# Expert rows added onto preset residual rows by the scatter DMA, and a final stage that reads one row per token in place of two

## The reference, cut to what matters

```python
x = _layernorm(x + _L0_attn_ref(x, ...), axis=-1)
x = _layernorm(x + _L0_xattn_ref(x, ctx_1024, _lenS2, ...), axis=-1)      # x2
x = _layernorm(x + _L0_ffn_ref(x, ...), axis=-1)

# _L0_ffn_ref
probs = jax.nn.softmax(xf @ router_w.T, axis=-1)
topv, topi = jax.lax.top_k(probs, 2)
probs = probs * mask                       # mask: 1 at topi, else 0
probs = probs / (probs.sum(axis=-1, keepdims=True) + 1e-09)
h = jax.nn.silu(g) * u                     # g, u: xf @ gate_w[e] + gate_b[e], xf @ up_w[e] + up_b[e]
expert_out = jnp.einsum('nef,efd->ned', h, down_w) + down_b
y = jnp.einsum('ne,ned->nd', probs, expert_out)
```

## Time and profile before

| What | us |
|---|---|
| median of 3 runs | 1800.53 |
| the profiled execution's own time | 1800.48 |
| its span (first to last instruction) | 1798.6 |
| expert stage's loop, first to last scatter issue | 1345.3 to 1748.7 |
| final stage, first load to last store's issue | 1756.0 to 1794.5 |

### The profile page before, as it was taken

The page is one execution under the profiler, slowest core; times in us unless marked ns, Lnnn a source line. Parts: engine busy times, 40 slices in busy tenths (PEclk is TensorE's granted clock), DMA queues, the critical chain, the costliest instruction groups (busy, mean ns, idle before and its releaser), DMA issues. The chain is left out here.

```text
span 1798.6 us, 30884 instructions
## 1 busy us (share of the span) xinstructions
PE 1530.3 (85%) x10698; PEld 1085.6 (60%) x10698; DVE 1113.7 (62%) x2342; ACT 744.4 (41%) x1630; POOL 660.0 (37%) x571
## 2 busy tenths in 40 slices
PE   6998982389999999985899999997559999999970
PEld 3554542378888888652677777776426666666650
DVE  5898892457777775560557777778525545555545
ACT  5666651024434443462555455452113333333324
POOL 1645435413223330100343565655423333333320
PEclk9998995579999999998999999999669999999995
DMA  3242326655556545143123113103301111111117
GB/s 101 82 163 82 135 110 141 166 120 131 135 144 162 150 121 178 58 154 129 56 82 106 44 60 126 36 25 106 141 21 45 45 48 46 45 48 45 48 36 280
DMA packets 188843, 177.73 MB, mean 99 GB/s; under 512 B 88359, under 2 KB 147419, under 8 KB 188571
## 3 DMA queue, kind: packets, MB, share of 16 engines
q1 hardware_dynamic: 174075, 148.70, 27.9%
q0 software_dynamic: 10400, 22.95, 3.9%
q10 hardware_dynamic: 4224, 4.19, 0.7%
HBM read 115.68 MB, written 60.11 MB: 98 GB/s over the span
## 5 line engine op out<-in xcount | busy, mean ns | idle before, releaser
L599 DVE SCALAR_TENSOR_TENSOR conv_y<-conv_in,taps,conv_y 128x512 f32<-128x512 f32 x192 | 184.2, 977 | 30.0 <-ACT conv_y L464 25.4
L2341 POOL DMA_INDIRECT y<-o,idx x71 | 83.3, 1173 | 242.0 <-DVE o L2484 234.2
L2420 ACT ACTIVATE xsT<-pX 128x256 f32<-128x256 f32 x71 | 27.2, 383 | 304.0 <-PE pX L2365 304.0
L2376 PE MATMUL pG<-w_gu,xsT 128*128 x284 | 135.5, 600 | 1.2 <-ACT xsT L2420 1.1
L2376 PE MATMUL pU<-w_gu,xsT 128*128 x284 | 134.7, 597 | 0.0
L2397 PE MATMUL pD<-late,hT 128*128 x568 | 134.2, 379 | 0.0
L1792 PE MATMUL xQ<-late,last 128*128 128x512 f32 x256 | 124.9, 610 | 8.9 <-ACT late L1948 4.8
L379 PE MATMUL ps_j<-xnT,w_qkv 128*128 128x512 f32 x256 | 128.7, 639 | 0.0
L1747 POOL TENSOR_TENSOR sc<-sc,den 128x1232 f32<-128x1232 f32 x32 | 72.0, 2249 | 109.2 <-DVE den L2168 109.1
L2397 PEld LDWEIGHTS pD<-late,hT 128*128 128x128 f32 x568 | 102.5, 190 | 11.0
L2480 DVE TENSOR_TENSOR o<-pD,late 128x256 f32<-128x256 f32 x71 | 30.2, 425 | 121.5 <-PE pD L2397 121.5
(11 more groups left out here) (338 smaller groups left out, 3640.8 us busy)
## 6 DMA issues: line engine op xcount, KB each, us to landing
qkvg<-tok SPq DMA_DIRECT2D x8, 2048.0 KB, 6.6
qkvg<-gate SPq DMA_DIRECT2D x8, 1024.0 KB, 9.0
steps<-step SPq DMA_DIRECT2D x32, 256.0 KB, 4.3
qks<-qkvg SPq DMA_DIRECT2D x32, 256.0 KB, 4.7
vb<-qkvg SPq DMA_DIRECT2D x32, 256.0 KB, 4.7
gt<-qkvg SPq DMA_DIRECT2D x32, 256.0 KB, 3.3
y<-y SPq DMA_DIRECT2D x16, 512.0 KB, 8.0
vw<-even SPq DMA_DIRECT2D x4, 1232.0 KB
```

The costliest lines, as they stand in the source:

```text
L599: y = nc.vector.scalar_tensor_tensor(conv_y[m % 4][:], conv_in[b][:, m, k:k + BT], taps[:, m, k:k + 1], conv_y[m % 4][:], ALU.mult, ALU.add)
L2341: nc.gpsimd.indirect_dma_start(out=s["y"].rearrange("t p d -> (t p) d"), out_offset=bass.IndirectOffsetOnAxis(ap=idx[j % 8][:, 0:1], axis= ...
L2376: mm = pe.matmul(to[:], xsT[q][:, c, :], w_gu[:, bass.ds(e, 1), c, k * FF:(k + 1) * FF], start=c == 0, stop=c == KD - 1)
```

## The change

A token's two expert rows go to the same row of `y`, which beforehand holds the residual. The scatter is issued with `compute_op=ALU.add`, so the DMA adds what it carries to what memory holds. The residual is put there in cross_stage by a second store of each x2 block. `kept` goes, with its ACT instruction and its semaphore, and DVE's last operation on `o` becomes a tensor_scalar. The entries of the padding get spare rows of their own, one for each expert, list tile and partition. The final stage loads one tile per block, has a buffer for each block, and needs no sum. Lines not shown change names, counts of semaphores, or remove the flag.

```diff
+SPARE = (NE * (P - 1) + NE * REGION + P - 1) // P
@@ delta_stage, SP and POOL
-                    sp.wait_ge(blank_set, 3)
+                    sp.wait_ge(blank_set, NE + 3)
...
-                    nc.gpsimd.tensor_scalar(blank[:, :, 1], con[:, C_COL:C_COL + 1].broadcast_to([P, NE * REGION]),
-                                            float(2 * TILES * P), None, ALU.add).then_inc(blank_set, 1)
+                    for e in range(NE):
+                        nc.gpsimd.tensor_scalar(blank[:, e * REGION:(e + 1) * REGION, 1],
+                                                con[:, C_COL:C_COL + 1].broadcast_to([P, REGION]), float(NE),
+                                                float(TILES * P + e * REGION), ALU.mult, ALU.add).then_inc(blank_set, 1)
...
+                    pool.wait_ge(blank_set, NE + 2)
+                    spare = blank[:, :, 1].rearrange("p (e n) -> p e n", e=NE)
+                    nc.gpsimd.tensor_tensor(spare, spare, con[:, C_IOTA:C_IOTA + REGION].unsqueeze(1).broadcast_to(
+                        [P, NE, REGION]), ALU.add).then_inc(blank_set, 1)
@@ cross_stage
+                sp.dma_start(y_v[n], x2t[:]).then_inc(x2_out, 16)
...
-            nc.gpsimd.memset(ent[:, :, 0, 3], 1.0).then_inc(set_up, 1)
...
-                                            float((k * TILES + t) * P), None, ALU.add).then_inc(set_up, 1)
+                                            float(t * P), None, ALU.add).then_inc(set_up, 1)
...
-                        dve.wait_ge(x2_out, n * 16)
+                        dve.wait_ge(x2_out, n * 32)
@@ expert_stage, POOL
-                    pool.wait_ge(kept_done, j - 3)
...
-                    in_=o[q][:], in_offset=None).then_inc(o_out[q], 16)
+                    in_=o[q][:], in_offset=None, compute_op=ALU.add).then_inc(o_out[q], 16)
@@ expert_stage, ACT
-            def residual(j):
-                if j >= 4:
-                    act.wait_ge(o_done, j - 3)
-                act.wait_ge(xs_in[j % 4], 16 * (j // 4) + 16)
-                nc.scalar.activation(kept[j % 4][:], xs[j % 4][:], ACT.Copy, scale=rows[j % 8][:, 3:4]
-                                     ).then_inc(kept_done, 1)
@@ expert_stage, DVE
-                dve.wait_ge(kept_done, j + 1)
                 dve.wait_ge(ob_done, j + 1)
-                nc.vector.scalar_tensor_tensor(o[r][:], o[r][:], rows[j % 8][:, 0:1], kept[r][:], ALU.mult, ALU.add
-                                               ).then_inc(o_done, 1)
+                nc.vector.tensor_scalar(o[r][:], o[r][:], rows[j % 8][:, 0:1], None, ALU.mult).then_inc(o_done, 1)
@@ final_stage
-        y = [sb(f"y7_{q}", [P, 2, BLK, D]) for q in range(4)]
-        z = [sb(f"z7_{q}", [P, BLK, D]) for q in N]
+        y = [sb(f"y7_{q}", [P, BLK, D]) for q in N]
...
-                if n >= 4:
-                    sp.wait_ge(z_sum, n - 3)
-                for k in range(2):
-                    sp.dma_start(y[n % 4][:, k], y_v[k, n]).then_inc(y_in[n], 16)
+                sp.dma_start(y[n][:], y_v[n]).then_inc(y_in[n], 16)
...
-                dve.wait_ge(y_in[n], 32)
-                nc.vector.tensor_tensor(z[n][:], y[n % 4][:, 0], y[n % 4][:, 1], ALU.add).then_inc(z_sum, 1)
-                dve.wait_ge(z_sum, n + 1)
+                dve.wait_ge(y_in[n], 16)
@@ build
-        "y": dram("y", [2 * TILES + 1, P, D]),
+        "y": dram("y", [TILES + SPARE, P, D]),
```

More of the change, by code:

```diff
@@ L1589, in cross_stage @@
         x2_v = s["x2"].rearrange("(n t) p d -> n p t d", t=BLK)
+        y_v = s["y"][0:TILES].rearrange("(n t) p d -> n p t d", t=BLK)
         con = s["con"]
@@ L1652, in cross_stage @@
         RIDE = 4 * KC + 8
-        SET_UP = 5 + 3 * BLK + NE + 1
+        SET_UP = 4 + 3 * BLK + NE + 1
         JOBS = {0: (3, 4, 5), 1: (6, 7), 2: (0,), 3: (1, 2)}
@@ L1705, in _ @@
             store_x2(BLOCKS - 1)
-            sp.wait_ge(x2_out, 16 * BLOCKS)
+            sp.wait_ge(x2_out, 32 * BLOCKS)
         @block.gpsimd
@@ L2295, in expert_stage @@
         hT = [sb(f"hT6_{q}", [P, FK, P]) for q in Q]
-        kept = [sb(f"kept6_{q}", [P, D]) for q in R]
         o = [sb(f"o6_{q}", [P, D]) for q in R]
@@ L2304, in expert_stage @@
         o_out = [sem(f"e_o_out{q}") for q in R]
-        (idx_done, xT_done, xT_sb, gu_done, gb_done, ub_done, silu_done, h_done, hT_done, hT_sb, d_done, kept_done,
-         ob_done, o_done) = [
+        (idx_done, xT_done, xT_sb, gu_done, gb_done, ub_done, silu_done, h_done, hT_done, hT_sb, d_done, ob_done, o_done) = [
             sem(f"e_{n}") for n in ("idx_done xT_done xT_sb gu_done gb_done ub_done silu_done h_done hT_done hT_sb "
-                                    "d_done kept_done ob_done o_done").split()]
+                                    "d_done ob_done o_done").split()]
         block = ctx.enter_context(nc.Block())
@@ L2448, in _ @@
                     silu(j)
-                    residual(j)
         @block.vector
@@ L2518, in final_stage @@
         y_in = sems("y_in")
-        set_up, st_done, mv_done, sd_done, r_done, sh_done, z_sum, z_done, z_out = [
-            sem(f"f_{n}") for n in "set_up st_done mv_done sd_done r_done sh_done z_sum z_done z_out".split()]
-        y_v = s["y"][0:2 * TILES].rearrange("(k n t) p d -> k n p t d", k=2, t=BLK)
+        set_up, st_done, mv_done, sd_done, r_done, sh_done, z_done, z_out = [
+            sem(f"f_{n}") for n in "set_up st_done mv_done sd_done r_done sh_done z_done z_out".split()]
+        y_v = s["y"][0:TILES].rearrange("(n t) p d -> n p t d", t=BLK)
         out_v = out.rearrange("b (c t p) d -> (b c) p t d", p=P, t=BLK)
@@ L2544, in finish @@
                 for t in T:
-                    last = nc.scalar.activation(z[n][:, t, :], z[n][:, t, :], ACT.Identity, bias=shift[n][:, t:t + 1],
+                    last = nc.scalar.activation(y[n][:, t, :], y[n][:, t, :], ACT.Identity, bias=shift[n][:, t:t + 1],
                                                 scale=rstd[n][:, t:t + 1])
@@ L2548, in finish @@
                 act.wait_ge(z_done, n + 1)
-                act.dma_start(out_v[n], z[n][:]).then_inc(z_out, 16)
+                act.dma_start(out_v[n], y[n][:]).then_inc(z_out, 16)
             for n in N:
@@ L2567, in _ @@
             for n in N:
-                dve.wait_ge(y_in[n], 32)
-                nc.vector.tensor_tensor(z[n][:], y[n % 4][:, 0], y[n % 4][:, 1], ALU.add).then_inc(z_sum, 1)
-                dve.wait_ge(z_sum, n + 1)
+                dve.wait_ge(y_in[n], 16)
                 for t in T:
-                    nc.vector.bn_stats(stats[n][:, t, :], z[n][:, t, :]).then_inc(st_done, 1)
+                    nc.vector.bn_stats(stats[n][:, t, :], y[n][:, t, :]).then_inc(st_done, 1)
                 dve.wait_ge(st_done, n * BLK + BLK)
```

## The result

The changed kernel took 1793.19 us in the median of 17 runs, the kernel before 1802.16 us in the median of 17 runs beside them. The ratio is 0.9949, with a 95% interval of 0.9936 to 0.9962. Timed again on another occasion, the same two kernels gave 0.9967 (0.9953 to 0.9981). The profiled execution has a span of 1790.0 us against 1798.6 us.

The account below looks back on a forecast made before the run. PE was taken to bound the expert loop, the order of waits the final stage. From 1800.48 us, -9.3 us (final stage) and +2.5 us (last scatters) gave 1793.7 us, range 1789.5 to 1799 us.

Parts of the forecast that it names:

- The final stage: Final stage: without the sums and second loads, the last store is issued 9.3 us earlier, with ACT as the bound.
- The scatter's x: Expert stage: additional time of a scatter that adds in memory, between 0 and 2.8 us, taken as 1.0 us.
- The three landings in a row: End of the expert loop: the last three scatters move the stage's end by 3x - 0.54, +2.5 us at x = 1.0.
- The rule of the Trainium skill: Adding scatter: an adding DMA needs two source reads on one ring, delivering about half the bytes; x about 1.0 us.
- No cost in the loop: Expert loop: PE stays full, the period stays 5.81 us, and x is hidden up to 1.96 us.
- No cost of the second store, the blank list and the lost work of ACT and DVE: Cross stage, delta stage and expert loop: added stores, POOL's list work and removed ACT and DVE work count 0.
- A sign of being wrong: Delta or cross stage: a shift by more than 1 us was to show that the prediction is wrong.
- the third rival: Adding scatter: x is about 0, 9.3 + 0.5 us at most off, 1790.6 us; chance 0.10.
- The sum: Whole kernel: -9.3 us from the final stage and +2.5 us from the tail, together -6.8 us.

Follow-up runs that it names:

- the doubled scatter: The changed kernel with each adding scatter issued twice, the second after the first has landed; one run, 2002.7 us.
- The halves: The kernel before with only the new final stage, ratio 0.9943; the changed kernel with the old final stage (two loads and DVE's sum), ratio 1.0011.

## Why the prediction was right, step by step

- **The final stage** was forecast at -9.3 us and gave -7.9 and -9.2 us in the two profiles of the changed kernel, and -9.7 us alone. By the means of four profiles each, 39.2 us before and 29.5 us with one row per token, it is -9.7 us. The start was right (7.8 us behind the first load, forecast 7.6), the distance a little pessimistic (2.72, forecast 2.83). What the step left out is that a store's issue can stand behind the loads: 2.24 us in one profile, 1.00 in the other. I had counted 0.43 us for each.
- **The scatter's x**, the additional time of an adding scatter, was taken as 1.0 us, from the moving part of the scatter and the gather. In the tail of the first profile it came out as 1.25 us in the first distance (5.10 against 3.85), 0.54 us in the second (4.39) and 0.7 us in the last landing (3.8 against 3.1), 0.83 us in the mean, and 0.6 us of it is POOL's longer issue. In the loop the median landing grew by 1.4 us, from 2.6 to 4.0 us, which the loop's period hid.
- **The three landings in a row** were to cost 3x - 0.54 = 2.5 us. In the first pair of profiles they cost 2.1 us: 8.07 us from the first to the last of the three scatters became 9.49, and the landing adds 0.7. But the base was not a fixed one. I took 3.85 us as what two plain scatters in a row need, and with plain scatters the first distance was 5.2 to 5.6 us in three of five profiles. By the means the three scatters went from 8.7 to 9.2 us apart and the last landing from 3.0 to 3.7 us, so this part cost 1.2 us and was forecast at twice that.
- **The drain** was missing. I wrote that the end of the stage moves by 3x - 0.54 and took what follows the landing as fixed; it grew by 1.4 us. This is the step that failed. That the tail still cost about what was forecast (2.6 us by the means, 2.5 forecast; 3.5 us in the first pair of profiles) is luck: the missing drain made up for the landings that were priced too high.
- **The rule of the Trainium skill** ("Collectives: The Full Stack", "The bandwidth ceiling: the fold count and why AG ≠ RS ≠ AR") is stated there for the reduce step of a collective over several cores, and no run here shows that case. Its direction holds for this scatter: the DMA engines' share in the loop rose from 0.15 to 0.29 at 46 GB/s, about twice the engine time for the same counted bytes. The additional reads are not among these bytes: the page of the profile shows 111.5 MB read from memory after and 115.7 MB before, and the 4.2 MB less are the eight loads. The time from issue to landing grew less than the engine time did, by 0.7 us of 3.1 for the last scatter and by 1.4 us of 2.6 in the loop.
- **No cost in the loop**: right, with a period of 5.81 us. The forecast put the distance at 3.85 + 1.0 = 4.85 us; the doubled scatter shows 4.3 us, so of the 5.81 us 1.5 us were left.
- **No cost of the second store, the blank list and the lost work of ACT and DVE**: the store alone measured 1.0001. For the list, POOL's operations ended 0.9 us after 726.72, before SP's issue at 728.66. From the first of these operations to SP's issue it is 5.81 us, and was 5.80 us before:

```profile
722.85 2.56 POOL L990 TENSOR_SCALAR blank<-con 128x33 f32<-128x33 f32 x8
725.48 1.16 POOL L993 TENSOR_SCALAR blank<-con 128x264 f32<-128x264 f32 x1
726.72 0.89 POOL L997 TENSOR_TENSOR blank<-blank,con 128x264 f32<-128x264 f32 x1
```

- **A sign of being wrong that was set too narrow.** I had called the prediction wrong if the delta or the cross stage shifts by more than 1 us. The cross stage started 4.3 us earlier in the first profile of the changed kernel, 1.2 us later in the second, and in the four kernels that are unchanged up to there it started between 816.3 and 819.3 us. The sign fired without saying anything about the change.
- **Two slips in the sums.** 21.8 us of DMA from 1756.0 end at 1777.8, not at 1779.5; ACT works longer either way. For x = 0 the scatter's step says 0.17 us of gain and the third rival counts 0.5 us, so its time would be 1791.0 us and not 1790.6.
- **The sum.** Forecast -6.8 us; the first two profiles of the changed kernel show -4.4 and -6.2 us against the first one before, the timed runs -9.2 (ratio 0.9949) and -5.9 us (0.9967). By the means of all profiles the final stage gives -9.7 us and the scatter costs 2.6 us: -7.1 us, a ratio of 0.9961, which lies inside the intervals of both timings, near the edge of the first. The first pair alone says less because its profile before has the shortest final stage and one of the shortest tails, and its profile after the longest of both. The halves, timed alone, measured 0.9943 and 1.0011, together 0.9954, between the two timings, so nothing points to a further effect of the change. Between the two timings the changed kernel's median moved by 4.3 us and its mean granted clock from 0.927 to 0.926. The clock goes with the time in the runs of one kernel, as shown above, but how much of the 4.3 us is its doing was not traced.

## What to carry to other kernels

To let a scatter add in memory is a trade between two stages: it costs at the end of the scattering stage, where landings stand in a row and POOL's drain grows, and pays in the stage that reads. Ask for every serial chain what its distance is against the period that hides it, and look at the stage's end separately, drain and barrier included, since the loop's average says nothing on it. When loads are moved ahead of a barrier, count what their issues cost the issuing engine: here the first four took 0.4 to 0.5 us each, the later ones up to 2.7 us. And before a difference of a few us is put down to a change, take several profiles of both sides: here the tail of the unchanged scatter alone differed by 1.4 us from one profile to the next, the start of the loop by 8.6 us.

## What the runs showed of the hardware that I had not expected

- POOL's drain at the end of the expert stage had the same length to the nanosecond in every kernel of a kind: 2999 ns in all five that scatter plainly, 4382 ns in all six that add, 5812 ns with 142 adding scatters. That is 1.4 us for each 71 adding ones. Why was not tried.
- The landing of a plain scatter at the end of the loop was not fixed: the last but two took 3.3 us in two profiles and 4.5 to 4.8 us in three, in kernels whose POOL does the same in the loop. With the adding scatter it took 3.9 to 4.4 us in six.
- The adding scatter moved its 128 KB in 144 packets where the plain one had 48, and the count of bytes stayed the same.
- In the final stage the first four loads of 512 KB took SP 0.38 to 0.51 us each to issue, the fifth 0.7 to 1.0 us and later ones up to 2.75 us. On ACT a store's issue took 0.38 to 0.47 us, but up to 2.24 us for the first one, behind the loads, and this delays the arithmetic behind it.
